# Gather passes of a four-layer GNN on one core: rows and records counted in fours

## The reference

```
h = relu(layernorm(x));  x = x + L0(h, edge_attr_3, src, dst)   # edge MLP, summed by dst
h = relu(layernorm(x));  x = x + L1(h, edge_index, edge_type_8) # 8 relations, summed by src
h = relu(layernorm(x));  x = x + L2(h, edge_index)              # attention by dst, 8 heads, batch norm
h = relu(layernorm(x));  x = x + L3(h, edge_index)              # degree-normed, summed by src
```

## Time and profile before

| | us |
|---|---|
| median of three runs | 5331.8 |
| span of the profiled execution (no other time of it is shown) | 7126.6 |
| GpSimd busy | 3826.6 (54%) |
| TensorE matmul busy | 4263.3 (60%) |
| VectorE busy | 3340.4 (47%) |
| ScalarE busy | 1440.5 (20%) |
| mean GB/s over the span | 76 |

### The profile page before, as it was taken

How to read it: one execution, slowest core, us unless ns; L and a number is a source line. 1 busy time by engine, 2 the same in 40 slices (tenths; PEclk the granted TensorE clock), 3 DMA queues, 4 the chain that set the end, 5 groups by cost and what they waited for, 6 DMA issues and landing times. The chain is left out here.

```text
span 7126.6 us, 113087 instructions
## 1 busy us (share of the span) xinstructions
PE 4263.3 (60%) x13279; PEld 2710.9 (38%) x13284; DVE 3340.4 (47%) x11588; ACT 1440.5 (20%) x4442; POOL 3826.6 (54%) x4006
## 2 busy tenths in 40 slices
PE   4324666667724434966665665777777764656665
PEld 1202333333313211434343334555566553434443
DVE  5124555666502101345555555555555564444444
ACT  0202333333312100100000002444444440000000
POOL 3465555555562574036666665555555525666665
PEclk7655766666656656976667676777766766776677
DMA  1112333333300101434444443333333324444443
GB/s 45 40 30 58 80 80 81 80 78 78 73 6 1 32 21 49 147 107 98 98 98 97 97 98 77 82 80 82 82 81 81 81 62 94 95 94 95 94 94 87
DMA packets 1059254, 541.25 MB, mean 76 GB/s; under 512 B 864525, under 2 KB 956238, under 8 KB 1058889
## 3 DMA queue, kind: packets, MB, share of 16 engines
q0 software_dynamic: 177920, 424.21, 21.2%
q1 hardware_dynamic: 507624, 90.64, 6.8%
q10 hardware_dynamic: 373600, 25.30, 3.3%
HBM read 449.78 MB, written 89.82 MB: 76 GB/s over the span
## 5 line engine op out<-in xcount | busy, mean ns | idle before, releaser
L1727 PE MATMUL psS_plain_src<-got_plain_src,hot_plain_src 128*128 x3328 | 1374.7, 561 | 982.0 <-SPq L1558 559.6
L1727 PEld LDWEIGHTS psS_plain_src<-got_plain_src,hot_plain_src 128*128 128x128 f32 x3328 | 828.0, 273 | 1477.6 <-issue 1356.1
L685 POOL DMA_INDIRECT got_attend_dst<-dram_gtab,recs_attend_dst x832 | 812.2, 976 | 643.3 <-DVE msg_attend_dst L766 300.1
L1601 DVE TENSOR_TENSOR sums<-sums,psS_plain_src 128x257 f32 x1664 | 700.8, 421 | 901.6 <-issue 412.4
L1576 POOL DMA_INDIRECT got_edge_mlp_dst<-dram_ptab,rows_i_edge_mlp_dst x784 | 741.8, 946 | 595.4 <-SPq L1555 402.1
L561 POOL DMA_INDIRECT dram_rec_src<-rec_src x784 | 765.7, 977 | 508.3 <-issue 245.4
L1576 POOL DMA_INDIRECT got_plain_src<-dram_xtab,rows_i_plain_src x784 | 746.7, 952 | 478.3 <-SPq L1555 292.1
L1576 POOL DMA_INDIRECT got_plain_src<-dram_htab,rows_i_plain_src x784 | 746.7, 952 | 456.0 <-SPq L1555 268.6
L1738 PE MATMUL psS_edge_mlp_dst<-msg_edge_mlp_dst,hot_edge_mlp_dst 128*128 128x256 f32 x1664 | 792.2, 607 | 173.2 <-DVE sage_sums L1601 89.0
L880 PE MATMUL psS_attend_dst<-msg_attend_dst,hot_attend_dst 128*128 128x264 f32 x1664 | 757.2, 549 | 41.1 <-issue 32.0
L1948 PE MATMUL psO_tab<-w_tab,hT_tab 128*128 128x512 f32 (+1 forms) x980 | 476.8, 636 | 348.7 <-DVE out_tab L1924 190.9
(11 more groups left out here) (366 smaller groups left out, 4563.9 us busy)
## 6 DMA issues: line engine op xcount, KB each, us to landing
dram_xtab<-out_tab SPq DMA_DIRECT2D x48, 1024.0 KB
recs_plain_src<-dram_rec_src ACTq DMA_DIRECT2D x1664, 4.0 KB
recs_edge_mlp_dst<-dram_rec_dst ACTq DMA_DIRECT2D x832, 4.0 KB
recs_attend_dst<-dram_rec_dst SPq DMA_DIRECT2D x832, 4.0 KB
got_attend_dst<-dram_gtab,recs_attend_dst POOLq DMA_INDIRECT x832
dram_rec_src<-rec_src POOLq DMA_INDIRECT x784
got_edge_mlp_dst<-dram_ptab,rows_i_edge_mlp_dst POOLq DMA_INDIRECT x784
got_plain_src<-dram_xtab,rows_i_plain_src POOLq DMA_INDIRECT x784
```

The lines of the kernel that those rows point to most:

```text
L685: nc.gpsimd.indirect_dma_start(got[:, u, 0:w], None, table, bass.IndirectOffsetOnAxis(rec_i[:, u, index_word:index_word + 1], 0)).then_inc ...
L1601: nc.vector.tensor_tensor(here, here, psS[t[1] % banks][:, 0:cols], ALU.add).then_inc(added, 1)
L1727: nc.tensor.matmul(psS[t[1] % banks][:, 0:cols], hot[:, t[1], :], flat[:, bass.ds(slots.of(u), cols)], start=True, stop=True).then_inc(sum ...
```

## The change

`AHEAD` goes. The 16 semaphores `rec_in` become 4, one for four neighbouring slots, and so do the 16 `row_in`; a wait asks for 64 (four DMAs of 16) per round. SyncE's relay in `pair_pass` runs once in four steps, with the wait for the pairs of the last of the four old tiles and one increment of `free`, and then the wait for the group of rows before and an increment of `landed` by 4; the `gate` increment goes. GpSimd waits for `free` at every fourth tile. In `edge_pass` SyncE and GpSimd wait at every fourth tile only, for all four tiles of the group, and VectorE waits for rows once in four tiles.

```
-AHEAD = 6
+FOUR = 4
 # edge_pass, sync
-                if (old := ring.at(i, u, U)) is not None:
-                    sp.wait_ge(row_in[u], 16 * (old[0] + 1))
+                if u % FOUR == 0 and (old := ring.at(i, u, U)) is not None:
+                    sp.wait_ge(row_in[u // FOUR], 16 * FOUR * (old[0] + 1))
                     gate.step()
                     sp.wait_ge(rels, fours(old))
                     gate.step()
-                sp.dma_start(rec[:, u, :], rec_d[bass.ds(off, P), :]).then_inc(rec_in[u], 16)
+                sp.dma_start(rec[:, u, :], rec_d[bass.ds(off, P), :]).then_inc(rec_in[u // FOUR], 16)
 # edge_pass, gpsimd
-                if (old := ring.at(i, u, U)) is not None:
-                    wait_count(pool, free, ring.count(old))
-                pool.wait_ge(rec_in[u], 16 * (t[0] + 1))
-                gate.step()
+                if u % FOUR == 0:
+                    if (old := ring.at(i, u + FOUR - 1, U)) is not None:
+                        wait_count(pool, free, ring.count(old))
+                    pool.wait_ge(rec_in[u // FOUR], 16 * FOUR * (t[0] + 1))
+                    gate.step()
 # edge_pass, vector
-                for s_ in range(u, u + 4):
-                    dve.wait_ge(rec_in[s_], 16 * (t[0] + 1))
+                dve.wait_ge(rec_in[u // FOUR], 16 * FOUR * (t[0] + 1))
...
-                        for s_ in (scores[1] - 1, scores[1]):
-                            dve.wait_ge(row_in[s_], 16 * (scores[0] + 1))
+                        if scores[1] % FOUR == 1:
+                            dve.wait_ge(row_in[scores[1] // FOUR], 16 * FOUR * (scores[0] + 1))
 # pair_pass, sync
+                if u % FOUR != FOUR - 1:
+                    return
                 if tiles.at(i, u) is not None and tiles.at(i, u, U) is not None:
-                    if u == 0:
+                    if u == FOUR - 1:
                         pairs_of.load(i)
                     sp.wait_ge(used, pairs_of.of(u))
-                    gate.step()
                     sp.sem_inc(free, 1)
-                if (t := tiles.at(i, u, AHEAD)) is not None:
-                    sp.wait_ge(row_in[t[1]], 16 * (t[0] + 1))
-                    sp.sem_inc(landed, 1)
-            tiles.run(sp, step, lag=AHEAD)
+                if (t := tiles.at(i, u, FOUR)) is not None:
+                    sp.wait_ge(row_in[t[1] // FOUR], 16 * FOUR * (t[0] + 1))
+                    sp.sem_inc(landed, FOUR)
+            tiles.run(sp, step, lag=FOUR)
 # pair_pass, gpsimd
-                if t >= U:
-                    pool.wait_ge(free, t - U + 1)
+                if t >= U and t % FOUR == 0:
+                    pool.wait_ge(free, (t - U) // FOUR + 1)
 # pair_pass, vector (begin) and scalar (spread_out)
-                for s_ in range(u, u + 4):
-                    dve.wait_ge(rec_in[s_], 16 * (t[0] + 1))
+                dve.wait_ge(rec_in[u // FOUR], 16 * FOUR * (t[0] + 1))
```

More of the change, by code:

```diff
@@ L603, in edge_pass @@
         gaps = sem("gaps")
-        rec_in = [sem(f"rec_in{s}") for s in range(U)]
-        row_in = [sem(f"row_in{s}") for s in range(U)]
+        rec_in = [sem(f"rec_in{g}") for g in range(U // FOUR)]
+        row_in = [sem(f"row_in{g}") for g in range(U // FOUR)]
         hots, sums, added, start = sem("hots"), sem("sums"), sem("added"), sem("start")
@@ L686, in step @@
                                              bass.IndirectOffsetOnAxis(rec_i[:, u, index_word:index_word + 1], 0)
-                                             ).then_inc(row_in[u], 16)
+                                             ).then_inc(row_in[u // FOUR], 16)
             ring.run(pool, step)
@@ L811, in step @@
                         k = t[1] % 4
-                        dve.wait_ge(row_in[t[1]], 16 * (t[0] + 1))
+                        dve.wait_ge(row_in[t[1] // FOUR], 16 * FOUR * (t[0] + 1))
                         wait_count(dve, sums, ring.count(t, 4))
@@ L863, in step @@
                         k = t[1] % 4
-                        act.wait_ge(row_in[t[1]], 16 * (t[0] + 1))
+                        act.wait_ge(row_in[t[1] // FOUR], 16 * FOUR * (t[0] + 1))
                         wait_count(act, sums, ring.count(t, 4))
@@ L1530, in _ @@
         def _(sp):
-            gate = Gate(sp, c.passed["sp"])
             pairs_of = Places(nc.sync, (done, 0), tiles, U, sh.NT, least=1)
@@ L1573, in _ @@
                     pool.wait_ge(rows_in[min(t, 1)], 16 * max(t // U, 1))
-                if t >= U:
-                    pool.wait_ge(free, t - U + 1)
+                if t >= U and t % FOUR == 0:
+                    pool.wait_ge(free, (t - U) // FOUR + 1)
                 nc.gpsimd.indirect_dma_start(got[:, t % U, 0:width], None, table,
-                                             bass.IndirectOffsetOnAxis(rows_i[:, t, :], 0)).then_inc(row_in[t % U], 16)
+                                             bass.IndirectOffsetOnAxis(rows_i[:, t, :], 0)).then_inc(row_in[t % U // FOUR], 16)
             scatter.run(pool)
@@ L1649, in _ @@
                     head.load(u // 4)
-                act.dma_start(rec[:, u, :], rec_d[bass.ds(head.of(u % 4), P), :]).then_inc(rec_in[u], 16)
+                act.dma_start(rec[:, u, :], rec_d[bass.ds(head.of(u % 4), P), :]).then_inc(rec_in[u // FOUR], 16)
             def fetch(i, u):
@@ L1660, in fetch @@
                             act.wait_ge(spreads, fours(old))
-                    act.dma_start(rec[:, t[1], :], rec_d[bass.ds(offs.of(u), P), :]).then_inc(rec_in[t[1]], 16)
+                    act.dma_start(rec[:, t[1], :], rec_d[bass.ds(offs.of(u), P), :]).then_inc(rec_in[t[1] // FOUR], 16)
             def spread_out(t):
-                for s_ in range(t[1], t[1] + 4):
-                    act.wait_ge(rec_in[s_], 16 * (t[0] + 1))
+                act.wait_ge(rec_in[t[1] // FOUR], 16 * FOUR * (t[0] + 1))
                 wait_count(act, turned, fours_before(t, 2))
```

## The result

The changed kernel takes 5350.83 us (median of 5 runs, 5348.11 to 5357.89); the kernel before took 5327.67 beside it (5 runs, 5324.65 to 5335.28). The ratio is 1.0036, interval 1.0025 to 1.0047: 19 us slower, between 13 and 25. The prediction said 5340, 8 us slower. The sign and the kind of cost (starts and ends of passes) came true, the size did not, because the largest term is missing from its sum.

What follows compares the result with a forecast made beforehand. The prediction took GpSimd's indirect DMAs, 1.25 us a gather, to bound the timed passes, with SyncE's relay waits absent. Starts 1.6 and ends 3 x 2 summed to 7.6 us on 5331.8: 5340 us, overall range 5235 to 5390, own range 5325 to 5352.

Steps and rivals of the forecast that it cites:

- Part 1: SyncE's relay in the pair passes: fewer instructions worth 0 off the profile, up to 963 us if the holds are real.
- The test by the median: Indirect DMAs at their floor, 4968 us, plus 920 us of other stretches already exceed the median, leaving waits no room.
- the rule of the Trainium skill: Trace-record writing pushes back when its buffers fill and can hold an engine; so the relay's stalls belong to the recording.
- The forecast of about 6500 us: Profiled span of the changed kernel: from 7126.6 to about 6500 us (6250 to 6900), as most of 963 us goes.
- Part 2: free and landed by fours in the pair passes: GpSimd never waits, 0; slack 3.2 us, 1.9 at a round's first group.
- Part 3: Fewer waits on VectorE, ScalarE and GpSimd: worth 0, at most 42 us if one of them were the bound.
- Part 4: Start of a pass: attention's first gather waits for four records and starts 1.6 us late; plain passes 0.
- Part 5: End of a pass: last four tiles freed at once, +2 us in each plain pass and attention, 0 in edge MLP.
- A: SyncE's holds in the pair passes are partly real, so fewer relay instructions gain: 5232 us (5180 to 5318); chance 0.30.
- B: The release of free queued behind the landing comes late, above all at a round's first group: 5384 us; chance 0.18.
- C: TensorE becomes the attention pass's bound if bursts lower its granted clock to 0.66: 33 us, 5373; chance 0.11.
- D: SyncE stays last in profiled passes, one held instruction delaying four tiles: profiled span near 7000, timed as forecast; no chance given.

Runs made afterwards that it cites:

- e1: The kernel before without the bookkeeping increment (gate.step) of SyncE's relay in the pair passes: 5329.95 us, ratio 0.9994.
- e8: The kernel before, unedited, recorded again on the slow chip: timed median 7059.87 us, recorded span 7059.6 us.
- after: The changed kernel, with the whole change against the kernel before: 5350.83 us, ratio 1.0036.
- e11: The changed kernel with SyncE's lag for relaying rows in the pair passes 8 steps in place of 4: 5335.68 us, ratio 1.0009 to before.
- e12: e11 with a row semaphore for each slot and rows handed on one tile at a time in the pair passes: 5323.8 us, ratio 0.9987 to before.
- e3: The kernel before with the change in the attention pass (edge_pass) alone: 5329.3 us, ratio 0.9997.
- e10: The kernel before, with GpSimd waiting for free only before every fourth gather of the pair passes, on a quick chip: 5336.59 us, ratio 1.0008.
- e2: The kernel before with the change in pair_pass alone: 5348.43 us, ratio 1.0031.
- e9: The changed kernel, unedited, run again on another quick chip: 5351.46 us, ratio 1.0041 to before.
- e4: e3 with a row semaphore for each slot in the attention pass, VectorE waiting for rows two tiles at a time: 5331.77 us, ratio 0.9995 to before.
- e5: The changed kernel with GpSimd waiting for free before every gather of the pair passes, on the slow chip: 7229.78 us, ratio 1.0240 to before.
- e7: The changed kernel with a row semaphore for each slot and rows handed on singly in the pair passes, slow chip: 7250.97 us, ratio 1.0287 to before.

## Why the prediction came out as it did

**Part 1, the relay's instructions: value right, reason wrong.** It held SyncE's long instructions for a product of the recording. The conclusion for the timed median (GpSimd's 1.25 us fill the passes, no wait for SyncE) is borne out: 983.8 / 783 = 1.256 us a gather in e1. The test by the median, 4968 + 920 us, pointed to the right place; what it told was that the recording and the three timed runs came from chips in different conditions. e8 bears that out, with a recorded span that equals the timed median of its chip and the clock and the holds of the first recording. For the rule of the Trainium skill that the prediction quoted (NOTIFIC — the notification-queue block, § 7.1 Overflow) no run here shows a case: the quick recordings have no holds at all (17/17/17 ns), and on the slow chip the timed runs are as long as the recorded ones. The forecast of about 6500 us for the profiled span fell with it: the recording was taken on a quick chip, 5346.3.

**Part 2, steady state: 0 predicted, some 12 to 18 us found. This is the step that failed.** Its times were nearly right. Rows are handed on 2.8 us after their last gather's start (median of 196 groups in each pair pass of after), the slack of the other groups is 3.3 us for 3.2. At a round's first group it is 1.1 for 1.9: from the relay of the rows to the release lie 2.4 us (2273.70 to 2276.10) in place of 1.53, with 1.13 for the threshold load in place of 0.94 and the rest in register operations, and the steps between them, that the sum left out. The larger fault is what was taken for enough. The prediction asked only whether the release comes before the gather starts. It does, and still four gathers in a pass start 1.4 to 1.8 us late: 5.8 and 6.1 us in the plain passes; the same four pauses, 5.8 us, stand in the MLP pass, where the quick recordings scatter by 13 us (984.0 to 997.5). e11, which gives the release more room, takes all but one small one away and 15 us with them. That the late release uncovers them is shown, and that they sit at fixed gathers. That three of the four also need the shared row semaphores, which the prediction took for a mere saving of waits, is what the slow chip's traces say; e12 doesn't part the two. What happens on GpSimd at each 208th gather is open; no run was made for it.

**Part 3, fewer waits:** worth 0, right (e3 0.9997, e10 1.0008).

**Part 4, attention's start:** 1.6 us predicted; 21.5 to 22.2 us from the last addition without it and 22.8 to 23.8 with it bear that out.

**Part 5, the ends:** 2 us in each plain pass predicted; 3.3 and 1.9 found to the last addition. Behind that of the last pass another 1.0 us goes: its last eight matmuls (L1439) take 2.07 and 1.11 us by fours where e1's take 1.13 and 1.03, at a granted clock of 0.66 (5329 to 5340 us) against 0.81 (5305 to 5316 in e1). 0 in the MLP pass, by the cover of 16 scatters: +3.9 found, the cover does not reach GpSimd's drain. 2 in the attention pass: from its last gather to the next first one are 107.0 to 107.4 us in e1, e2 and e10 and 108.6 to 109.7 in e3, after, e9, e11 and e12, so 1 to 2.7; e4, which counts attention's rows singly, has 107.3. Together 4 and 5 come to 14.7 us (3.9 + 5.3 + 2.6 + 2.9 in the table) where 7.6 were forecast.

**Luck.** 5350.83 lies in the forecast's own range, 5325 to 5352. That range allowed for ends of 3 to 4 us each, and the sum has no pause in it, so the number lies there by luck.

**The rivals.** A, the holds are partly real and the relay gains: on the slow chip they are in the timed runs, and even there a quarter of the relay gains nothing (e5, e7); on a quick one they don't exist. Refuted on both, as far as e5 and e7 stand for the change. Its price was also added up loosely: one eighth of 963 is 120, and cheaper waits can only add to that, yet the sum takes 100. B, the release queued behind the landing: the right place, a round's first group, and half of the mechanism. The release is late, but never so late that GpSimd waits for it, and the landing stayed at 2.8 us, where B needed 4.8. An excess was priced at 44 us on 147 first groups; what was found is about 18 us of pauses at 12 of them. B was given 0.18. Its sign was to be a wait of GpSimd for L1555, and in the plain passes that sign never showed: the loss stands under "issue". C, TensorE through its clock: attention's clock is 0.87 and its 832 gathers take 1066.8 us, as in e1. Refuted. D: on a quick chip the relay never was last; on the slow one e7's 92 long waits are what D describes.

## What to carry over

Where a relay serves two directions in one queue, put the hand-back of free slots ahead of the wait for arrivals by a whole group more than the arithmetic asks: moving one lag from 4 to 8 was worth 15 us of 5350. Merge what is off the path at its cheapest end only: giving each slot its own row semaphore again and handing rows on one by one was worth another 12 us (e12 against e11). And before a long or odd instruction time is put down to the recorder, compare the recorded span with timed runs of the same chip, and with a recording on another: here 7059.6 and 7059.87 agreed, a second chip's recording had no holds, and the puzzle was between two chips.

## What the runs showed beside that

One kernel took 7059.87 us on one chip and about 5333 on the others; on the slow one SyncE's register operations reached 1.4 us (median 23 ns) and its increments 0.7 (median 17), and the granted clock was 0.679 in place of 0.785. What holds the instructions there is not known. A gather that itself waits for nothing can be up to 1.77 us late with no releaser in the profile, at numbers 113, 321, 529 and 737 of a pass, and then starts 3.74 to 3.80 us behind a release that the gather before it asked for. And the first gathers of the attention pass take longer in every recording, seven of them 1.62 us or more in place of 0.95 (most 1.63, one up to 2.55), as these of after:

```profile
3156.24 0.94 POOL L686 DMA_INDIRECT got_attend_dst<-dram_gtab,recs_attend_dst  x1 [29.34 <-DMA recs_attend_dst<-dram_rec_dst]
3157.49 1.63 POOL L686 DMA_INDIRECT got_attend_dst<-dram_gtab,recs_attend_dst  x1 [0.30 <-DMA recs_attend_dst<-dram_rec_dst]
3159.42 1.63 POOL L686 DMA_INDIRECT got_attend_dst<-dram_gtab,recs_attend_dst  x1 [0.30 <-issue]
```
